# Three-product scores and cross projections, loads in groups, and eight steps moved to other PSUM banks, in a fused decoder layer

## The reference

```
x = LN(x + selfattn(x))      # 16 query heads of 64, 4 key/value heads, rotary, alibi slopes,
                             # scores = q k^T / 8 + slope * (j - i), softmax, @ v, @ Wo
x = LN(x + crossattn(x, ctx))# 16 heads of 16, layer norm before q, k, v and the output
                             # projection, rotary, windows of 64 that see themselves and the
                             # one before, masked by order and by equal cell number
x = LN(x + ffn(x))           # gate, up: 256 -> 1024 and down: 1024 -> 256, weights ternary,
                             # activations rounded to 8 bits, silu(gate) * up
```

## Time and profile before

| | us |
|---|---|
| median of 3 runs (2326.09 to 2327.27) | 2327.14 |
| the profiled execution | 2328.01 |
| its span, first to last instruction | 2326.2 |
| PE busy in the span | 2229.3 (96%) |
| DVE busy | 1976.2 (85%) |
| ACT busy | 1568.7 (67%) |
| POOL busy | 1220.2 (52%) |

### The profile page before, as it was taken

How to read it: one execution, slowest core, us unless ns; L and a number is a source line. 1 busy time by engine, 2 the same in 40 slices (tenths; PEclk the granted TensorE clock), 3 DMA queues, 4 the chain that set the end, 5 groups by cost and what they waited for, 6 DMA issues and landing times.

```text
span 2326.2 us, 54958 instructions
## 1 busy us (share of the span) xinstructions
PE 2229.3 (96%) x18218; PEld 1644.8 (71%) x18218; DVE 1976.2 (85%) x8167; ACT 1568.7 (67%) x4449; POOL 1220.2 (52%) x1390
## 2 busy tenths in 40 slices
PE   5899999999999999999999999999999999999974
PEld 4666677777777777777777777777777777777752
DVE  5778888888888888888888888888888888888865
ACT  2477666777766777767677766677776667776741
POOL 2445555555555555565555555555556555555531
PEclk8899999999999999999999999999999999999997
DMA  5000110110011111011011001111101111100100
GB/s 169 27 11 24 28 36 26 35 36 23 23 36 35 27 36 30 18 34 36 27 35 35 22 24 35 34 28 35 31 15 35 35 27 35 36 22 23 36 10 14
DMA packets 84662, 74.69 MB, mean 32 GB/s; under 512 B 18336, under 2 KB 79136, under 8 KB 84384
## 3 DMA queue, kind: packets, MB, share of 16 engines
q1 hardware_dynamic: 84384, 71.19, 11.3%
HBM read 45.98 MB, written 8.39 MB: 23 GB/s over the span
## 4 chain that ended last, share of the span: by engine, by line
PE 83%; DVE 9%; ACT 3%; POOL 2%; issue 2%; SPq 1%; DMA 1%; DVEq 0%; POOLq 0%; ACTq 0%
PE bank L444 20%; PE bank L456 11%; PE bank L539 9%; PE bank L558 9%; PE bank L462 9%; PE bank L569 8%; PE bank L610 3%; PE bank L636 3%; PE bank L617 3%; PE bank L688 2%; PE bank L449 2%; PE bank L665 2%; PE bank L675 2%; POOL qx_tok L1200 2%; DVE q_sin L858 1%
## 5 line engine op out<-in xcount | busy, mean ns | idle before, releaser
L1177 POOL TENSOR_TENSOR prob<-prob,precs 128x512 f32<-128x512 f32 x512 | 542.9, 1076 | 381.9 <-DVE precs L821 381.8
L1092 ACT ACTIVATE prob<-prob,nmax 128x256 f32<-128x256 f32 x1024 | 508.2, 498 | 260.1 <-DVE nmax L814 260.1
L814 DVE CUSTOM_DVE_ANT_0 prob<-bank,alibi 128x256 f32<-128x256 f32 x1024 | 372.8, 420 | 63.7 <-PE bank L539 58.9
L1099 ACT COPY pT<-bank 128x512 f32<-128x512 f32 x512 | 298.7, 583 | 143.9 <-PE bank L444 143.9
L1116 ACT ACTIVATE px<-px,nmx 128x128 f32<-128x128 f32 x1024 | 314.0, 392 | 70.0 <-DVE nmx L919 70.0
L444 PE MATMUL bank<-ident,prob 128*128 128x128 f32 x2048 | 316.6, 277 | 10.1 <-ACT pT L1099 8.4
L444 PEld LDWEIGHTS bank<-ident,prob 128*128 128x128 f32 x2048 | 237.7, 141 | 79.1 <-issue 43.7
L539 PE MATMUL bank<-kk,qq 64*128 64x256 f32 x2048 | 291.9, 404 | 0.7 <-DVE nmax L814 0.7
L919 DVE CUSTOM_DVE_ANT_0 px<-bank,mask 128x128 f32<-128x128 f32 x1024 | 225.7, 284 | 44.2 <-PE bank L617 32.6
L558 PE MATMUL bank<-pT,v_sb 128*64 128x256 f32 x2048 | 249.3, 385 | 0.0
L539 PEld LDWEIGHTS bank<-kk,qq 64*128 64x128 f32 x2048 | 177.5, 187 | 55.1 <-issue 34.7
(11 more groups left out here) (194 smaller groups left out, 5004.1 us busy)
## 6 DMA issues: line engine op xcount, KB each, us to landing
xT<-in_xT SPq DMA_DIRECT2D x32, 256.0 KB, 4.1
kx_tok<-in_ctx SPq DMA_DIRECT2D x32, 256.0 KB, 3.7
cT<-in_ctxT SPq DMA_DIRECT2D x32, 256.0 KB, 2.8
xtok<-in_x SPq DMA_DIRECT2D x32, 256.0 KB, 3.0
kx<-k_sin SPq DMA_DIRECT2D x256, 32.0 KB, 2.0
vs<-vx SPq DMA_DIRECT2D x64, 128.0 KB, 2.5
out_y<-y SPq DMA_DIRECT2D x32, 256.0 KB, 2.2
cellk<-in_cell SPq DMA_DIRECT2D x32, 64.0 KB, 3.7
```

The lines of the kernel that those rows point to most:

```text
L814: v.tensor_tensor_reduce(out=prob[:, (2 * p + q) % SLOTS, c, :], in0=psum[SCORES[c]][:, q * L:(q + 1) * L], in1=alibi[:, p % 2, c, :], sca ...
L1092: nc.scalar.activation(prob[:, (2 * p + q) % SLOTS, c, :], prob[:, (2 * p + q) % SLOTS, c, :], ACT.Exp, bias=nmax[:, i:i + 1], scale=-1.0, ...
L1099: nc.scalar.copy(pT[:, p % 2, :, :, q * P:(q + 1) * P].rearrange("p c k n -> p (c k) n"), bank[:].rearrange("p (c n) -> p c n", c=4)).then ...
L1177: g.tensor_tensor(prob[:, n % SLOTS, :, :], prob[:, n % SLOTS, :, :], precs[:, 2 * n:2 * n + 2].unsqueeze(2).to_broadcast([P, 2, L]), ALU. ...
```

## The change

1. **Scores in three products.** `kk` and `qq` become pairs of float32r tiles. ACT writes the high parts (`kk_hi`, `qq_hi`), and DVE gets a new instruction in `kT` and in each of the four `qT`. PE makes 12 products in a step `S` in place of 4. One alibi table serves both heads of a pair; the other factor goes into a scale by partition (`q_scale`).
2. **Cross projections in three products.** Weights are split once in `prep 4`. `yT` and `noT` become pairs (new DVE instruction in `NX` and `NO`), the context becomes `c_hi` (new ACT step `C`) and `c_lo` (new POOL step `C`). `KP` and `VP` are merged into `KV 0` and `KV 1`, one token tile each with keys and values side by side in 512 columns.
3. **Banks.** `OX` and `BX` (four steps) move from bank 7 to 5, `HT` and `D` (four steps, since `D` is now one per token tile) to 6.
4. **Engines.** `HC` moves from DVE to POOL, `X2` and `out` from DVE to ACT, which need `f_bias` and `z_bias` from POOL (two small instructions more each). The two half-width rotations of `K` and `Q` on DVE become one instruction.
5. **Loads in groups.** The projection weights come in three groups of 512 columns, each split as it lands; the rope table, the alibi table and `gb` have semaphores of their own, and `prep 0` waits for `gb` alone. PE, not SP, adds the initial credits.
6. **Shared tiles**: `xT` and `cT` are one tile `raw`, `y` is `xtok`, `y2` is `x1`, `y3` is `x2`, `o_tok` is `qx_tok`; `hqT`, `by_sin` and `qq` hold fewer copies.
7. `HEAD`, `BODY` and `TAIL` are new orders. `BODY` still runs 27 times with lags of 0 to 4.

```
-                        for q in range(2):
-                            for c in range(2):
-                                half = slice(c * HD, (c + 1) * HD)
-                                last = mm(psum[SCORES[c]][:, q * L:(q + 1) * L], qq[half, u, m, q * P:(q + 1) * P],
-                                          kk[half, p // 4, :], start=True, stop=True)
+                        parts = ((qq_hi, kk_hi), (qq_lo, kk_hi), (qq_hi, kk_lo))
+                        for q in range(2):
+                            for i, (qs, ks) in enumerate(parts):
+                                for c in range(2):
+                                    half = slice(c * HD, (c + 1) * HD)
+                                    last = mm(psum[SCORES[c]][:, q * L:(q + 1) * L], qs[half, u % 2, m, q * P:(q + 1) * P],
+                                              ks[half, p // 4, :], start=i == 0, stop=i == 2)
...
             def by_token(xs, ws):
+                parts = ((xs[0], ws[0]), (xs[1], ws[0]), (xs[0], ws[1]))
                 for t in range(TT):
-                    for k in range(KT):
-                        last = mm(psum[7][:, t * D:(t + 1) * D], xs[:, k, t * P:(t + 1) * P], ws[:, k, :], start=k == 0, stop=k == KT - 1)
+                    for i in range(KT * 3):
+                        k, (x, w) = i // 3, parts[i % 3]
+                        last = mm(psum[7][:, t * D:(t + 1) * D], x[:, k, t * P:(t + 1) * P], w[:, k, :], start=i == 0, stop=i == KT * 3 - 1)
...
+                    elif kind == "KV":
+                        t, = args
+                        pe.wait_ge(*at("c_lo", b))
+                        pe.wait_ge(*freed(sem, bank, part, place, it))
+                        parts = ((c_hi, wkvx_hi), (c_lo, wkvx_hi), (c_hi, wkvx_lo))
+                        for i in range(KT * 3):
+                            k, (xs, ws) = i // 3, parts[i % 3]
+                            last = mm(psum[bank][:], xs[:, k, t * P:(t + 1) * P], ws[:, k, :], start=i == 0, stop=i == KT * 3 - 1)
...
+                    elif kind == "kT":
+                        dve.wait_ge(*at("k_hi", b))
+                        v.tensor_tensor(kk_lo[:], bank[:].rearrange("p (h n) -> p h n", h=2), kk_hi[:].bitcast(F32), ALU.subtract)\
+                            .then_inc(sem["k_ready"], 1)
+                    elif kind == "qT":
+                        u, = args
+                        dve.wait_ge(*at("q_hi", b, u))
+                        v.scalar_tensor_tensor(out=qq_lo[:, u % 2, :, :], in0=bank[:].rearrange("p (m n) -> p m n", m=2), scalar=q_scale[:, u:u + 1],
+                                               in1=qq_hi[:, u % 2, :, :].bitcast(F32), op0=ALU.mult, op1=ALU.subtract).then_inc(sem["q_ready"], 1)
...
+                    elif kind == "NX":
+                        dve.wait_ge(*at("yT_hi", b))
+                        v.tensor_tensor(yT_lo[:], bank[:].rearrange("p (k n) -> p k n", k=KT), yT_hi[:].bitcast(F32), ALU.subtract)\
+                            .then_inc(sem["yT_ready"], 1)
...
+                    elif kind == "C":
+                        act.wait_ge(*landed("ctxT_loaded", b))
+                        act.wait_ge(*at("KV_mm", b - 1, 1))
+                        nc.scalar.copy(c_hi[:], cT[:]).then_inc(sem["c_hi"], 1)
+                    elif kind == "X2":
+                        act.wait_ge(*landed("stored", b - 1))
+                        act.wait_ge(*at("f_bias", b))
+                        for t in range(TT):
+                            ins = nc.scalar.activation(x2[:, t, :], y2[:, t, :], ACT.Identity, bias=f_bias[:, t:t + 1], scale=f_rstd[:, t:t + 1])
+                        ins.then_inc(sem["x2_ready"], 1)
...
+                    elif kind == "HC":
+                        t, = args
+                        pool.wait_ge(*at("hq_shift", b, t))
+                        pool.wait_ge(*at("HT_mm", b, t - 1))
+                        g.tensor_scalar(hq[:], hh[:, t, :], MAGIC, 127.0, ALU.subtract, ALU.min).then_inc(sem["hq_ready"], 1)
```

A stretch of the new `BODY` of which the prediction speaks:

```
+    (1, 'R', 6), (1, 'R', 7), (1, 'O', 0), (2, 'NX'), (3, 'G', 0), (3, 'U', 0), (1, 'T', 4), (1, 'qT', 2), (2, 'QX'),
+    (3, 'G', 1), (3, 'U', 1), (1, 'T', 5), (0, 'K'), (3, 'G', 2), (3, 'U', 2), (2, 'QXT'), (1, 'qT', 3),
+    (1, 'load_ctxT'), (1, 'C'), (1, 'load_ctx'), (1, 'T', 6), (1, 'S', 4), (2, 'SX', 0), (0, 'Q', 0, 1), (1, 'T', 7),
```

More of the change, by code:

```diff
@@ L177 @@
-    ("PO",): ("y2_ready", 0), ("XQ",): ("xqT_ready", 0), ("D",): ("y3_ready", 0),
+    ("load_xT",): ("x_lo", 0), ("load_ctxT",): ("c_lo", 0), ("KXT",): ("kxT_ready", 0), ("NO",): ("noT_ready", 0),
+    ("PO",): ("y2_ready", 0), ("XQ",): ("xqT_ready", 0),
 }
@@ L189 @@
 EMPTIED.update({("HT", t): ("hqT_ready", t) for t in range(TT)})
+EMPTIED.update({("D", t): ("y3_ready", t) for t in range(TT)})
+EMPTIED.update({("KV", t): ("vx_ready", t) for t in range(TT)})
 def holds(kind, bank):
-    return bank in (XSCORES if kind == "SX" else SCORES if kind == "S" else (BANKS.get(kind),))
+    return bank in (XSCORES if kind == "SX" else SCORES if kind == "S" else (RAW,) if kind in ("load_xT", "load_ctxT") else (BANKS.get(kind),))
 FILL = max(x[0] for x in BODY) + 1
@@ L267, in build @@
         minus_half = sb("minus_half", [P, 2 * TT])
-        xT = sb("xT", [P, KT, L])
+        raw = sb("raw", [P, KT, L])
+        xT = raw
+        cT = raw
         x_hi = sb("x_hi", [P, KT, L], F32R)
@@ L373, in _ @@
         def _(sp):
-            for dst, src in first_loads:
-                sp.dma_start(dst, src).then_inc(proj_loaded, 16)
-            for name, n in COUNT.items():
-                sp.sem_inc(sem[name], CREDIT * n)
             def one(ap, b):
@@ L384, in run @@
                     kind, args = step[0], step[1:]
-                    if kind == "loads":
-                        g, = args
-                        if g == 2:
-                            sp.wait_ge(pre_dve, W_SPLIT)
+                    if kind == "first":
+                        i, = args
+                        for k in range(KT):
+                            sp.dma_start(raw_w[k][:, 512 * i:512 * i + 512], a["wqkv"][k * P:(k + 1) * P, 512 * i:512 * i + 512])\
+                                .then_inc(first_loaded[i], 16)
+                    elif kind == "tables":
+                        g, = args
+                        for dst, src in tables[g]:
+                            sp.dma_start(dst, src).then_inc(tables_loaded[g], 16)
+                    elif kind == "loads":
+                        g, = args
+                        if g == 0:
+                            sp.dma_start(gb[:].rearrange("p c k -> p (c k)"), a["gb"]).then_inc(gb_loaded, 16)
+                            sp.wait_ge(w_split, 12)
+                        elif g == 2:
+                            sp.wait_ge(pre_dve, P_CROSSED)
                         for dst, src in later_loads[g]:
@@ L497, in run @@
                     bank = BANKS.get(kind)
-                    if kind == "wo_ready":
+                    if kind == "first":
+                        pe.wait_ge(w_split, 4 * args[0] + 4)
+                    elif kind == "wo_ready":
                         pe.wait_ge(wo_split, 2)
@@ L683, in run @@
                     elif kind == "D":
-                        pe.wait_ge(*at("hqT_ready", b, 1))
+                        t, = args
+                        pe.wait_ge(*at("hqT_ready", b, t))
                         pe.wait_ge(*freed(sem, bank, part, place, it))
-                        for t in range(TT):
-                            for k in range(IC):
-                                last = mm(psum[bank][:, t * D:(t + 1) * D], hqT[:, t, k, :], wd16[:, k, :],
-                                          start=k == 0, stop=k == IC - 1)
+                        for k in range(IC):
+                            last = mm(psum[bank][:, 0:D], hqT[:, k, :], wd16[:, k, :], start=k == 0, stop=k == IC - 1)
                         last.then_inc(sem["D_mm"], 1)
+            for name, n in COUNT.items():
+                pe.sem_inc(sem[name], CREDIT * n)
             pe.wait_ge(pool_consts, POOL_CONSTS)
-            pe.wait_ge(pre_dve, W_SPLIT)
             run(HEAD)
@@ L772, in run @@
                     bank = psum[BANKS.get(kind, 0)]
-                    if kind == "wo_split":
+                    if kind == "first":
+                        i, = args
+                        cols = slice(512 * i, 512 * i + 512)
+                        dve.wait_ge(first_loaded[i], 16 * KT)
+                        for k in range(KT):
+                            v.tensor_copy(w_hi[:, k, cols], raw_w[k][:, cols]).then_inc(w_split, 1)
+                        for k in range(KT):
+                            dve.wait_ge(w_split, 4 * i + k + 1)
+                            v.tensor_tensor(w_lo[:, k, cols], raw_w[k][:, cols], w_hi[:, k, cols].bitcast(F32), ALU.subtract).then_inc(w_split, 1)
+                    elif kind == "tables":
+                        dve.wait_ge(tables_loaded[args[0]], 16 * len(tables[args[0]]))
```

(43 more changed lines are left out.)

263 lines of the change are left out of this document (126 added, 137 removed), and 181 rows, old and new, of tables (BODY, HEAD, TAIL).

## The result

The changed kernel takes 2437.9 us (median of 4 runs, 2437.7 to 2440.1) against 2327.1 of the kernel before on the same chip (4 runs): a ratio of 1.0479, 95% interval 1.0461 to 1.0497. The forecast was 2263. It is slower by 111 us, and 175 us from the forecast.

The account below looks back on a forecast made before the run. The prediction took PE, busy without gaps in the steady state, as the bound. PE's list -2.6 and new idle +0.7 gave -1.9 us an iteration, 31 times -59, with the start -64: 2263 us from 2327.1, range 2240 to 2290.

Parts of the forecast that it names:

- The products: PE's matmuls: `S` -1.2 us, cross projections -1.5, `D` +0.1, together -2.6 us an iteration.
- The lower 0.85 us for `S`: PE's score step: the low price for `S`, with float32r products at a quarter of the float32 time.
- Rival (c): Score steps on PE: half-array products don't run side by side (2446 us) or loads don't hide (2406); chance 0.10.
- DVE: DVE's work an iteration: +0.8 us, to 61.1 us of 66.1, leaving 5.0 us free.
- POOL gets two `HC` at about 1.13 (as L1233) ... Both hide behind PE: POOL and ACT: about 4.4 us more on POOL, under 3.5 on ACT, all fitting into their idle time.
- without that cover they would delay a `T` by at most 1.1 us: PE's transposes `T`: the most that the work added to ACT and POOL would delay one if not hidden.
- I take 0.7 us of new PE idle: PE in each iteration: 0.7 us of new waiting, all behind DVE's new subtractions, out of a possible 4.8 us.
- rival (d): PE: starts of the new steps and their bank waits eat the gain; within 5 us of 2327; chance 0.05.
- The banks by themselves cost PE nothing: The moved banks: no cost to PE and no work removed; they only allow another order.
- The start, "net -5 us": Before the loop: first `Q` 10 us earlier, splitting the cross weights about 5.5 us; net -5 us (-12 to +2).
- The end: After the last batch's reduction: about 1 us added by moved instructions, about that given back by `D` in halves; 0.
- gain in the loop that didn't come: The iterations: -1.9 us each, to 66.8 us, counted 31 times, -59 us.

Follow-up runs that it names:

- g1: The changed kernel with `HC` on POOL as a multiply by one and an add of -MAGIC, without the clamp at 127: 2360.4 us.
- e1: The changed kernel with `HC` back on DVE, nothing else: 2443.6 us.
- e7: The kernel before with `HC` on POOL in the dear form (subtract and min), old order: 2337.4 us.
- i1: `g1` with the scores' products in one float32 product again, copies and subtractions kept: 2381.2 us.

## Why the prediction was wrong

- **The products: right.** `S` 0.91 (forecast 0.91), `KV` 1.49 (1.49), `PO` 1.50 (1.41 to 1.56). The lower 0.85 us for `S`, from a quarter of the float32 price, is shown by no run. The half-array products run side by side and their loads hide. By the load rule of the Trainium skill ("TensorE: Matmul & The Clock Gate", section "LDWEIGHTS (loading the stationary operand)", with the overlap as under "The mechanism") the prediction estimated 1.55 for `S`; the trace, with 0.91, doesn't agree. Rival (c) ended at 2406 to 2446, where the result lies, but by a mechanism that is shown false.
- **DVE: right.** 356.65/400 x 68.6 = 61.2 us an iteration in `g1` (forecast 61.1).
- **"POOL gets two `HC` at about 1.13 (as L1233) ... Both hide behind PE": wrong, the largest failed step.** The row was that of another operation. With 3.64 the time is 2437.9, with 1.17 it is 2360.4: 77.5 of the 175 us. "Hide behind PE" failed with the price: PE waited 35.9 us for `hq` and 31.8 us for `prob`. The sentence "without that cover they would delay a `T` by at most 1.1 us" fell with it. POOL was at 65%, and its spare time didn't help: what counts is that `HC` lies between `HS` and `HT` of its own batch and ahead of `R` on POOL's queue. DVE's spare time, 5.0 us by the prediction, didn't help either: `HC` put back there (`e1`) costs 83 us more than the cheap one on POOL. That the dear `HC` cost the steady state nothing in the old order (`e7`) shows that the price alone is not the cause either; price and new order together are. Which part of the new order makes it so was not found.
- **"I take 0.7 us of new PE idle": too low.** In `g1` PE is idle for 11.34/400 x 68.6 = 1.9 us an iteration, where it was 0.3: 1.6 of new idle. None of the waits that the profile names stands behind DVE's new subtractions, where the prediction had all of them: in 400:800 of `g1` PE waits 3.4 us for ACT's copies of `T`, 2.1 for the cross scores (`nmx`), 1.7 and 1.6 for rotations (`qx`, `by_sin`). The rest of the missing gain is that PE's busy time fell by only 1.7 us (68.4 to 66.7 an iteration) and not by 2.6. Summed by the distance of starts over 16 iterations, the products gave 2.5 of the 2.7 us forecast (scores 8.59 to 7.24, cross projections 7.18 to 6.02, which the prediction had at 7.45 before). But transposes and feed-forward products, which multiply the same as before, take 24.7 us in the new order for 23.9. `i1` shows besides that a shorter PE list is worth about half its length here. From the first to the last reduction `g1` gains nothing (2115.8 for 2115.0) where 59 us were forecast. This is nearest to rival (d), in which starts and bank waits eat the gain, though it is the old steps that start late.
- **"The banks by themselves cost PE nothing": not a term that can be separated.** PE waited 26.3 us for bank 6 (`nmx`), 15.1 with the cheap `HC`; undone under the new order, they cost 305 us.
- **The start, "net -5 us": wrong in sign,** +33.5 us. I had the first `Q` at 15 us; it came at 23.40. The diff said that PE adds the credits, and I gave the 117 increments no price. Nor did I follow SP's queue: the ternary loads now stage where the cross weights lie, so they wait for `prep 4` and then for `kx_clear`.
- **The end: right,** 33.7 us for 32.2, where no change was forecast. The step before it was not: the last two reductions are 58.7 us apart (61.7 in `g1`) for 54.0, and the prediction counted this stretch at PE's price. It is part of the loop's term below.

Sum of the misses: 77.5 (`HC`) + 59.8 (gain in the loop that didn't come) + 38.5 (start) = 175.8, against 174.9 us. The terms come from different runs, and the end's 1.5 us are left out, so a match this close is partly luck. What would have shown it wrong did: PE at 94% in the steady state, and its waits name ACT and POOL.

## What to carry to other kernels

Price an instruction that moves to another engine by a row of the same operation and operand kind on that engine, or leave its price open over a wide range; a probe at the end of a kernel, where nothing else runs, measures it in one run. An engine at 60% is not cover: look at what stands between the moved instruction and its reader, and what stands behind it on its queue. And where a loop's order is packed for given durations, banks and buffers, part of a change taken alone, or one step moved, can cost more than the whole change did.

## What the runs showed of the hardware

- On POOL a `tensor_scalar` of 128x1024 float32 took 1.17 us as multiply by a column and add, 2.8 us as one subtract or one min by an immediate, 3.67 us with both; on DVE the latter took 1.055. The Trainium skill says in "GPSIMD Engine Reference", section "Engine selection", that elementwise work with one input is roughly at line rate there; the 1.17 is near DVE's 1.055 and fits that, the 3.67 doesn't.
- A semaphore increment took (18.5 - 0.8)/116 = 0.15 us on PE's queue; on SP, in the kernel before, 108 of them took 6.7 us, 0.06 each.
- The twelve products of a score step on half rows, each with its own load of 128 columns (0.18 us long), start in pairs 0.12 us apart: the loads add no time to the products here.
- In 50:100 of the changed kernel PE was busy for 27.4 us and its granted clock was 0.72, a mix of the levels 2.4 and 1.2 GHz; before, busy for 41.8 us, it was 0.86. In 0:50 it was the other way round: 0.93 with 21.3 us busy, 0.90 with 24.3 before.
